# A drain of GpSimd after each group of eight gathers, in the edge stages of the first and third graph layers

## The reference

```python
x = layernorm(x + L0(x))   # attention, 4 heads: softmax over each target's edges
                           # of leaky(src_score[src] + tgt_score[dst]), then the
                           # weighted sum of proj[src]; proj = x @ W_proj
x = layernorm(x + L1(x))   # mean of (x @ W_msg.T)[src] per target, self term, relu, layernorm
x = layernorm(x + L2(x))   # e = leaky(ei[dst] + ej[src]); softmax over the edges of one SOURCE;
                           # sum of alpha * x[src] per target, relu
x = layernorm(x + L3(x))   # max over each target's edges of x[src] @ W[type] + b[type], self term
```

## Time and profile before

| | us |
|---|---|
| time, median of 3 runs | 4590.77 (4589.56 to 4595.85) |
| span of the profiled execution | 5974.2 |
| POOL busy in it | 3220.8 (54%) |
| PE busy | 2467.8 (41%) |
| DVE busy | 2086.7 (35%) |
| ACT busy | 830.0 (14%) |

### The profile page before, as it was taken

One profiled execution on the slowest core, in us unless ns is written; L12 is line 12 of the kernel. 1 busy time (PEld: TensorE's weight loads), 2 busy tenths in 40 slices (PEclk: granted clock), 3 DMA queues, 4 the chain that ended last, 5 costly groups with the idle time before them and its releaser, 6 DMA issues. The chain is left out here.

```text
span 5974.2 us, 63099 instructions
## 1 busy us (share of the span) xinstructions
PE 2467.8 (41%) x16441; PEld 2221.3 (37%) x16441; DVE 2086.7 (35%) x5443; ACT 830.0 (14%) x2496; POOL 3220.8 (54%) x3391
## 2 busy tenths in 40 slices
PE   2344444444333333332766666454566222222221
PEld 1333333333233333331666666344455222222220
DVE  4344434444122222222444344355544122222223
ACT  0111212122000000000322222000001011001112
POOL 3555555554566666664344444545443666666664
PEclk7555555555555555555555555566666556555555
DMA  4222222222122222223333333455555344434443
GB/s 102 57 60 60 61 58 60 59 61 57 41 47 47 47 49 47 48 47 63 115 110 108 107 108 115 130 162 162 162 164 160 93 117 116 108 108 112 112 116 82
DMA packets 427122, 543.15 MB, mean 91 GB/s; under 512 B 116266, under 2 KB 291966, under 8 KB 426862
## 3 DMA queue, kind: packets, MB, share of 16 engines
q1 hardware_dynamic: 311618, 311.80, 17.7%
q0 software_dynamic: 108064, 223.63, 16.6%
q10 hardware_dynamic: 7344, 6.61, 0.4%
HBM read 403.82 MB, written 142.41 MB: 91 GB/s over the span
## 5 line engine op out<-in xcount | busy, mean ns | idle before, releaser
L523 POOL DMA_INDIRECT G<-table,IC x2496 | 2362.6, 947 | 1571.7 <-issue 832.5
L2412 POOL DMA_INDIRECT G<-table,IC x448 | 433.1, 967 | 580.9 <-ACT IC L2271 425.1
L2818 DVE TENSOR_TENSOR_SCAN GW<-BIG,GW,PS 128x512 f32<-128x512 bf16 x208 | 266.2, 1280 | 962.9 <-DMA BIG<-run_mask 620.8
L2412 POOL DMA_INDIRECT G<-table2c,IC x384 | 367.3, 956 | 407.0 <-DMA rows_ahead<-G 148.8
L2780 PE MATMUL PS<-IDENT,GW 128*128 128x128 f32 x840 | 192.5, 405 | 862.3 <-issue 481.4
L1360 PE MATMUL PS<-SEL,G 128*128 128x96 f32 x1664 | 372.1, 417 | 358.1 <-DVE SEL L556 217.1
L1032 PE MATMUL PS<-SEL,GW 128*128 128x96 f32 x1664 | 382.4, 419 | 291.6 <-DVEq L1095 158.9
L1360 PEld LDWEIGHTS PS<-SEL,G 128*128 128x128 f32 x1664 | 359.7, 327 | 365.5 <-DVE SEL L556 220.1
L2780 PEld LDWEIGHTS PS<-IDENT,GW 128*128 128x128 f32 x840 | 158.9, 215 | 887.3 <-issue 495.6
L1032 PEld LDWEIGHTS PS<-SEL,GW 128*128 128x128 f32 x1664 | 356.4, 322 | 304.3 <-DVEq L1095 165.3
L2426 PE MATMUL PS<-BIG 128*128 128x49 f32 x1680 | 387.4, 408 | 60.7 <-issue 31.8
(11 more groups left out here) (314 smaller groups left out, 3749.1 us busy)
## 6 DMA issues: line engine op xcount, KB each, us to landing
rows_ahead<-G SPq DMA_DIRECT2D x104, 520.0 KB
running_max<-BIG SPq DMA_DIRECT2D x105, 512.0 KB
G<-table,IC POOLq DMA_INDIRECT x2944
GW<-source_in_block SPq DMA_DIRECT2D x160, 256.0 KB
ROWSF<-edge_places SPq DMA_DIRECT2D x209, 192.0 KB
BIG<-run_mask SPq DMA_DIRECT2D x104, 256.0 KB
ROWSF<-rows_ahead SPq DMA_DIRECT2D x26, 520.0 KB
SELTF<-rows_ahead SPq DMA_DIRECT2D x26, 520.0 KB
```

Source lines behind the costliest of these rows:

```text
L523: pool.indirect_dma_start(out=G[:, b, u, 0:width], out_offset=None, in_=table, in_offset=bass.IndirectOffsetOnAxis(ap=IC[:, b * U + u:b * ...
L2412: pool.indirect_dma_start(out=GS[:, b, u, 0:width], out_offset=None, in_=table, in_offset=bass.IndirectOffsetOnAxis(ap=IC[:, b * U + u:b * ...
L2818: v.tensor_tensor_scan(RM[:, q, h * 512:(h + 1) * 512], MB[:, q, h * 512:(h + 1) * 512], PS[2 * q + h][:], before, ALU.min, ALU.max).then_ ...
```

## The change

POOL gets a `drain` after the eight gathers of each group in `edges0` and in both halves of `layer2`. `edges1`, `edges3` and the fallback stages `edges2v_wide`, `edges2v_near` and `edges2`, which call `gather_rows` or `gather_group` too, stay as they are. A drain makes the queue of its engine wait until the engine has finished what was issued before.

```diff
-        def gather_rows(pool, table, width, indices_ready, opened, gathered, used, ahead):
+        def gather_rows(pool, table, width, indices_ready, opened, gathered, used, ahead, settle=False):
...
                         gather_group(pool, table, width, b, gathered)
+                        if settle:
+                            g.drain()
...
                 def _(pool):
-                    gather_rows(pool, T0, D + H, ic_ready, opened, gathered, rows_used, 0)
+                    gather_rows(pool, T0, D + H, ic_ready, opened, gathered, rows_used, 0, settle=True)
...
                                 out=GS[:, b, u, 0:width], out_offset=None, in_=table,
                                 in_offset=bass.IndirectOffsetOnAxis(
                                     ap=IC[:, b * U + u:b * U + u + 1], axis=0)).then_inc(gathered[b], 16)
+                            g.drain()
```

## The result

The changed kernel takes 5172.87 us (median of 3 runs, 5170.56 to 5174.58) against 4590.77: 1.124 of it, interval 1.117 to 1.131, 582 us slower. The forecast was 4664. The direction was right and the size was eight times too small.

The account below looks back on a forecast made before the run. POOL's gather issue was taken to bound layer 0 and layer 2's second half. At 0.48 us a drain, 50 (layer 0) + 0 (first half) + 23 (second half) = 73 us, 4591 + 73 = 4664 us; range 4570 to 4702.

Parts of the forecast that it names:

- POOL sets the pace of layer 0 and of layer 2's second half: Layer 0 and layer 2's second half: POOL's gather issue sets the length, 1037 and 479 us, with 9 us left for waiting.
- The ledger of 4582 us: Whole kernel: stage lengths without the stall, 413 us outside gathers included, sum to 4582 us against 4591 measured.
- The price of a drain, 0.48 us: Group boundaries in layers 0 and 2: the gap grows from 0.30 to 0.78 us, as set-up can't be done ahead.
- rival 5: Drained boundaries: the drain waits until rows have landed, 2.44 us each, 5047 us in all; chance 0.04.
- The first half covers its drains: Layer 2's first half: four gathered groups take 41.8 us with drains, under the sums' 43.6, so cost 0.
- The cover of 52 us: Layer 2's first half: POOL's idle time under the slower sums, 3.7 us in 43.6, hides 52 us of drain cost.
- Rival 1: Layer 2's second half: its consumers set the pace, so only layer 0 pays 50 us, 4641 us; chance 0.10.
- rival 2: Group boundaries: only the drain's own 0.08 us shows, set-up still done ahead, 12 us, 4603 in all; chance 0.07.
- Rival 6: All of layer 2 exposed, 4691 us, or a gap above 0.7 us, 4712 us at 0.8; chance 0.06.
- Rival 3 (hidden): Layer 0 and layer 2's second half: quicker unprofiled gathers leave POOL idle time that hides drains, 4591 us; chance 0.14.
- Rival 4 (faster): Gathering stages: pauses dissolve a stall also present in timed runs; 18% of 634 us saves 114, 4550 us; chance 0.17.
- Reading the stall as the profiler's load: All gather passes: other engines nearly standing still was put to the profiler, whose span was 1383 us above the timed median.

Follow-up runs that it names:

- the wait by semaphore: Changed kernel with each drain replaced by POOL waiting on the group's own semaphore until its eight gathers' rows have landed: 5135.17 us, 1.120 of the kernel before.
- each single-stage run: Changed kernel with drains kept in one stage only: layer 0 alone 4883.53 us (1.065), layer 2 alone 4876.04 us (1.064), against 4587.3 before.

## Why the prediction was wrong

- **POOL sets the pace of layer 0 and of layer 2's second half: right** on the chips of the timed runs. POOL's median gap was 0.31 us at all boundaries, and layers 0, 1 and 3 took 1043.1, 1046.9 and 1038.3 us for the predicted 1037.
- **The ledger of 4582 us closed partly by luck.** What lies outside the gathers is 323 us and not 413; the first half of layer 2 took 639.5 and not 579, the second 491.7 and not 479. Errors of -90 against +60 and +13, and 17 in layers 0, 1 and 3, cancelled. The outside stretches had been taken at the length they have in a stalled profile.
- **The price of a drain, 0.48 us: this is the step that failed.** The prediction took the drain's own end from the earlier trace rows, 0.08 us behind a memset. There no gather was in flight. Behind gathers the drain waits until the rows have landed: 1.7 us from the eighth gather's end to DVE's start, and 1.2 from there to the next gather, a gap of 2.93 instead of 0.30. The landing in rival 5 was sized rightly: 1.96 us against 1.92 in the mean of the four places in layer 0 (1.70, 1.61 and 1.71 at three, 2.67 at the one of 320.65). The rival had the mechanism and gave 2.44 us a boundary where layer 0 paid 2.86; it was given 4 in 100, because I took the one drain in the trace for the typical one. The rest of 0.4 us lies in the restart: 1.26 us in the mean of the four places where the prediction had 0.79, and 0.87 with the wait by semaphore. In the second half a drain cost 0.9 us more than 2.44; why there so much isn't shown.
- **The first half covers its drains: wrong.** It paid 131 us for 56 drains. The cover of 52 us was the difference of two paces, 43.6 and 39.9 us, and POOL's real pace there is slower than 39.9: in the kernel before the 448 gathers are busy for 467.7 us, 1.044 each, against 0.95 in layer 0, and with the gap of 0.31 a turn of four groups takes 43.3 us. So POOL had no idle time turn by turn; its gap at the boundaries was 0.31 us in the median already. All that it idled was the one wait for ACT at the start, 32.3 us, of which the drains of the first groups took up 18 (14.2 are left).
- **Rival 5's total of 5047 us** missed by 126. By stage it had 254, 85 and 117 us where 297, 131 and 160 were paid: it kept that cover of 52 us in the first half and had the drain in the other two too cheap by 43 us each.
- **Rival 1** (the second half is paced by its consumers) is out, since that half grew by 160 us, and **rival 2** by the gap of about 3 us. **Rival 6** had all of layer 2 exposed and a gap above 0.7 us; both came true, but it priced the gap at 0.8 us at most. **Rival 3 (hidden)** is refuted for quick chips by each single-stage run. **Rival 4 (faster)** is real, on the other kind of chip. Its price, 18% of 634 us saved, was far too small: layer 0 and the second half, at 1314.8 and 641.9 us, lost all of the stall, but they also pay for drains at the full price. Reading the stall as the profiler's load was wrong; the kernel before takes 5978 us when it is merely timed on such a chip.

## What to carry over

Before a drain behind DMAs is priced, ask what is in flight: on POOL it holds the queue until the last transfer issued has landed, plus a restart, and on the engine that sets the pace this is paid in full, here 2.3 to 3.3 us each. If an order is needed, and the group before is enough for it, wait for that group by semaphore; that cost nothing (1.000). And when a profile is a third longer than the timed runs, profile again before building on its stretches: here the two came from conditions under which the sign of the change is not the same.

## What the runs showed of the hardware that I had not expected

- The same program took 4587 us on two chips and 5976 to 6066 on three others. Of the 1391 us between the two profiles of the kernel before, 1301 lie in the five gathering stretches and 90 outside them. After some ten gathers without a pause PE, DVE and ACT nearly stood still while POOL kept its 1.25 us a gather, and SP issued no transfer from 1117.5 to 1139.9. Pauses of about 3 us after each eighth gather removed the stall from layer 0 and the second half of layer 2. Why, and what it is that jams, stays open. One thing the traces do say: part of PE's idle time is then no wait for rows or for another engine that the profile can name. Before its 98 weight loads and 98 matmuls of L784 (the same work in both) it idled 267.4 us, in 170 gaps that the profile puts to no releaser ("issue"); on the quick chip it was 2.4 us in 15 gaps. The first row is from the first profile, the second from the second:

```profile
  issue: 267.4, 170
```

```profile
  issue: 2.4, 15
```

- A second drain right behind the first costs nothing that the time shows (5173.22 against 5172.87 us).
- In layer 2's first half a gather is busy for 1.044 us in the mean instead of 0.95. On the quick chip 166 of the 448 take more than 1.0 us, and 94 of these overlap DVE's L2515, which only 3 of the others do. Writing that instruction in the longer form did not shorten the gathers on stalling chips (1.013 and 1.015 us in the mean against 0.965), and on a quick chip it wasn't tried, so the cause is open.
